# Expert outputs with queries on partitions, router weights as per-partition scalars on VectorE

## What is computed

```python
logits = x @ w_gate                       # 8 experts
w      = top-2 weights, 0 for the others  # one number per token and expert
h      = silu(x @ w1[e]) * (x @ w3[e])    # layers 0, 1, 3 (gated); gelu(x @ up[e]) in layer 2
y     += w[:, e:e+1] * (h @ w2[e])        # layer 3 also adds w @ bias
x      = x + y
```

## Time and profile before

| | |
|---|---|
| median of 3 runs | 4386.78 us |
| the profiled execution, its own time | 4390.38 us |
| its span, first to last instruction | 4388.7 us |
| TensorE busy | 4072.2 us, 93% |
| ScalarE busy | 3859.5 us, 88% |
| VectorE busy | 2842.1 us, 65% |
| GpSimd busy | 819.4 us, 19% |
| mean granted TensorE clock | 0.963 of full |

### The profile page before, as it was taken

The page is one execution under the profiler, slowest core; times in us unless marked ns, Lnnn a source line. Parts: engine busy times, 40 slices in busy tenths (PEclk is TensorE's granted clock), DMA queues, the critical chain, the costliest instruction groups (busy, mean ns, idle before and its releaser), DMA issues.

```text
span 4388.7 us, 69705 instructions
## 1 busy us (share of the span) xinstructions
PE 4072.2 (93%) x26742; PEld 975.0 (22%) x26742; DVE 2842.1 (65%) x5746; ACT 3859.5 (88%) x4328; POOL 819.4 (19%) x705
## 2 busy tenths in 40 slices
PE   8899999999999999999999999899999999999996
PEld 3122222222222222222212222222122221222212
DVE  6889887888977788677503232110685768988813
ACT  3699998999988989898998888889999888999993
POOL 3000003221033211333321111111001110021222
PEclk7699999999999999999999999999999999999998
DMA  5211011100011110111102121110011100010001
GB/s 145 62 29 35 25 31 42 30 18 15 12 47 41 29 30 25 49 35 35 36 16 64 41 64 37 50 41 25 12 29 30 29 15 13 15 35 24 9 6 54
DMA packets 124486, 151.35 MB, mean 34 GB/s; under 512 B 29272, under 2 KB 76384, under 8 KB 124080
## 3 DMA queue, kind: packets, MB, share of 16 engines
q1 hardware_dynamic: 123424, 146.41, 12.6%
q10 hardware_dynamic: 720, 0.40, 0.0%
HBM read 123.21 MB, written 23.51 MB: 33 GB/s over the span
## 4 chain that ended last, share of the span: by engine, by line
PE 58%; ACT 18%; DVE 13%; issue 4%; DMA 1%; SPq 1%; POOL 0%; ACTq 0%; POOLq 0%; DVEq 0%
PE av L1282 24%; ACT prob L1443 14%; PE scores L1272 12%; DVE mpart L1554 9%; PE side L1304 8%; PE scores L1382 5%; PE side L1400 4%; DVE above L1558 2%; PE side L1382 2%; PE scores L1295 1%; ACT above L1451 1%; PE side L1272 1%; DMA cwb<-weights 1%; PE scores L1420 1%; PE scores L1424 0%
## 5 line engine op out<-in xcount | busy, mean ns | idle before, releaser
L1443 ACT ACTIVATE prob<-scores 128x1024 f32<-128x1024 f32 x2999 | 2908.5, 1034 | 180.6 <-PE scores L1272 104.1
L1554 DVE TENSOR_REDUCE mpart<-side 128x1 f32<-128x512 f32 (+1 forms) x3456 | 2077.4, 655 | 451.6 <-PE side L1304 441.5
L1282 PE MATMUL av<-prob,VB 128*9 128x512 f32 x6528 | 873.6, 608 | 0.7 <-ACT prob L1443 0.5
L1282 PE MATMUL av<-prob,VA 128*9 128x512 f32 x6528 | 864.2, 602 | 1.2 <-ACT oS L1461 0.4
L1304 PE MATMUL side<-KA,QP 32*128 32x512 f16 (+1 forms) x2112 | 596.4, 394 | 62.8 <-DVE mpart L1554 39.7
L1272 PE MATMUL scores<-QP,KA 32*128 32x512 f16 x2998 | 577.0, 391 | 46.6 <-ACT prob L1443 30.3
L1272 PE MATMUL scores<-QP,KB 32*128 32x512 f16 x3000 | 573.6, 386 | 33.0 <-ACT prob L1443 19.9
L1558 DVE CUSTOM_DVE_ANT_0 above<-side,above 128x512 f32<-128x512 f32 x768 | 503.6, 687 | 154.0 <-PE side L1304 137.2
L1304 PE MATMUL side<-KB,QP 32*128 32x512 f16 (+1 forms) x2112 | 541.7, 380 | 59.3 <-DVE mpart L1554 32.6
L1451 ACT ACTIVATE above<-scores 128x1024 f32<-128x1024 f32 x383 | 394.4, 1030 | 70.5 <-DVE mpart L1558 41.9
L1272 PEld LDWEIGHTS scores<-QP,KB 32*128 32x128 f16 x3000 | 139.2, 91 | 808.1 <-ACT prob L1443 688.9
(11 more groups left out here) (216 smaller groups left out, 2674.0 us busy)
## 6 DMA issues: line engine op xcount, KB each, us to landing
cwb<-weights SPq DMA_DIRECT2D x80, 256.0 KB, 3.8
KA<-kstacks SPq DMA_DIRECT2D x384, 48.0 KB
KB<-kstacks SPq DMA_DIRECT2D x384, 48.0 KB
Fin<-in_Fin SPq DMA_DIRECT2D x64, 256.0 KB, 2.7
kstacks<-hi SPq DMA_DIRECT2D x100, 128.0 KB, 2.4
ctxc<-in_ctxT SPq DMA_DIRECT2D x36, 256.0 KB, 3.1
hT<-in_mask SPq DMA_DIRECT2D x16, 400.2 KB, 3.5
kstacks<-lo SPq DMA_DIRECT2D x50, 128.0 KB, 2.6
```

The source lines that it names most:

```text
L1282: last = pe.matmul(AV[ROWS * h:ROWS * h + VC, :], V[l % 2][:, kt, g * HG + h, :], prob[:, (e + h // 2) % RING, (h % 2) * QB:(h % 2) * QB + ...
L1443: act.activation(prob[:, e % RING, :], pair.rearrange("p a b -> p (a b)"), ACT.Exp if softmax(l) else ACT.Sigmoid, scale=SCALE).then_inc(s ...
L1554: dve.tensor_reduce(part, bank, AX.X, ALU.max).then_inc(sem["red"], 1)
```

## The change

The downward matmul swaps its operands: a tile of 128 queries of the hidden activations is held and the 128 columns of `Fout` are streamed, four times for the 512 queries, so that `y` has queries on partitions. The router's weight is then one number per partition, and VectorE multiplies and adds straight into the state, in all passes. `cwput`, `cwget`, `xk`, `hscale`, `gatec`, `yc`, `yT`, `yadd` and the buffer in DRAM go. The factor 0.5 moves into the router's small instructions. `cwT` and `cwTc` stay in layer 3 alone, for the biases, which become a product and an addition of their own behind the third expert. The upward matmuls no longer wait for the router: its steps are listed behind the upward steps of the second expert, and the first three fetches of weights ahead of the logits. The last finish takes score banks for the first half of its upward products. The planner's table gains costs for the new steps, and the finish of unit 6 is due at key tile 170 instead of 200. The diff also lets a phase go without differences of key chunks (`DIFS_IN`), but sets two for every phase, as before.

```diff
                 elif s.what == "down":
-                    pe.matmul(bank, Fout[0:fs, w, c, :], h, start=first, stop=c == nk - 1).then_inc(sem["bgP"], 1)
+                    for t in range(QT):
+                        last = pe.matmul(bank[:, t * P:(t + 1) * P], h[:, t * P:(t + 1) * P], Fout[0:fs, w, c, :], start=c + t == 0, stop=(c, t) == (nk - 1, QT - 1))
+                    last.then_inc(sem["bgP"], 1)
+                elif s.what == "bias":
+                    for t in range(QT):
+                        last = pe.matmul(bank[:, t * P:(t + 1) * P], cwT[:, t * P:(t + 1) * P], b2d[:], start=True, stop=True)
...
                 elif s.what == "ysum":
-                        dve.tensor_tensor(yT, yT, bank, ALU.add).then_inc(sem["bgV"], 1)
-                elif s.what == "yadd":
+                    own.wait_ge(*o.sem("routed", u, lp))
+                    for t in range(QT):
+                        last = dve.scalar_tensor_tensor(x[:, t, :], bank[:, t * P:(t + 1) * P], cw[:, t, k:k + 1], x[:, t, :], ALU.mult, ALU.add)
...
-                    if l in (0, 1) and j >= nk:
-                        own.wait_ge(*o.sem("xk", u, lp, k))
-                        x = xk[:, k % 2, :]
+                    own.wait_ge(*o.sem("xTc", u, f"r{lp}" if l == 1 else "f"))
...
+    behind = 1 if f["gated"] else 2
+    for k in range(E + behind):
         for j in range(n):
+            if k < E:
+                out += gated(k, j) if f["gated"] else upward(k, j)
+            if k >= behind and not f["gated"] and not by_dve(u, lp):
+                out += down(k - behind, j)
+        if k == 1:
+            out += route
+        if k >= behind and (f["gated"] or by_dve(u, lp)):
+            out += [s for c in range(n) for s in down(k - behind, c)]
+        if not f["gated"] and k < E and k % 2:
+            out += [Step("ACT", "gelu", (u, lp, i)) for i in (k - 1, k)]
+        if l == 3 and k == BIAS_AT + 1:
+            out += [Step("PE", "cwT", (u, lp)), Step("ACT", "cwTc", (u, lp)), Step("PE", "bias", (u, lp)), Step("DVE", "badd", (u, lp))]
...
+def last_steps():
+
+    return [s._replace(home="pair") if s.what == "up" and s.key[3] < FFN[3]["nk"] else s for s in finish_steps(7)]
...
-FFN_FROM, FFN_TO, KV_FROM, KV_TO = 12, [130, 130, 180, 180, 130, 130, 200], 24, 280
+FFN_FROM, FFN_TO, KV_FROM, KV_TO = 12, [130, 130, 180, 180, 130, 130, 170], 24, 280
```

More of the change, by code:

```diff
@@ L333, in pass_steps @@
-    for k in range(W_RING):
-        out.append((0, Step("SP", "wexp", (u, lp, k))))
-    out.append((0, Step("SP", "cwget", (u, lp, 0))))
-    if f["gated"] and l != 3:
-        out.append((0, Step("POOL", "xk", (u, lp, 0))))
-    out.append((16, None))
-    n = f["nk"]
+    n = f["nk"]
+    out = [Step("SP", "wexp", (u, lp, k)) for k in range(W_RING)] + [Step("PE", "logit", (u, lp))]
+    route = [Step("DVE", what, (u, lp)) for what in ("routea", "routeb", "routee", "routef", "routeg", "routeh")]
@@ L434, in finish_steps @@
         for g in range(NG):
-            out += [(1, Step("PE", "qproj", (u, g))), (0, Step("ACT", "qsplit", (u, g))), (0, Step("POOL", "qadd", (u, g)))]
+            out += [Step("PE", "qproj", (u, g)), Step("ACT", "qsplit", (u, g)), Step("POOL", "qadd", (u, g))]
     else:
-        out.append((2, Step("SP", "out", (b,))))
-    return out
-def placed(at, steps, taken, pace=1.0, together=False):
-    out = []
-    beat = at
-    for gap, s in steps:
-        at += gap
-        if s is not None and s.eng == "PE":
-            if together and s.what == "down" and s.key[-1]:
-                at = before + 4
-            else:
-                at = max(at, int(beat))
-                at += (1 - at) % 4
-                n = FFN[unit(s.key[0])[0]]["nk"] if together and s.what == "down" else 1
-                while any(at + 4 * i in taken for i in range(n)):
-                    at += 4
-                taken.update(at + 4 * i for i in range(n))
-            before = at
-            beat = max(beat, at - 4 * pace) + 4 * pace
-        if s is not None:
-            out.append((at, s))
+        out.append(Step("SP", "out", (b,)))
     return out
@@ L691, in next_maxima @@
         self.p = left[0] if left else None
-        n = len(HALVES[0])
-        self.single = [deque(range(0, n)), deque(range(n, FIRST_BOTH))]
-        self.both, self.dif, self.issued = [deque(), deque()], 0, 0
+        if left:
+            self.single = [deque(singles_of(self.p, half)) for half in range(2)]
+            self.difs, self.singles = deque(difs_of(self.p)), sum(len(x) for x in self.single)
+            self.both, self.issued, self.begun = [deque(), deque()], 0, 0
     def ready(self, s):
-        t = 0.0
-        for k in steps_before(s):
-            if k in self.todo:
-                if k not in self.done:
-                    return None
-                t = max(t, self.done[k])
+        name, t = (s.what, s.key), 0.0
+        if name not in self.before:
+            self.before[name] = [k for k in steps_before(s) if k in self.todo]
+        for k in self.before[name]:
+            if k not in self.done:
+                return None
+            t = max(t, self.done[k])
         return t
@@ L736, in engines @@
                     start = max(best[0], self.free[e])
-                    w = "both" if s.what == "red" and s.key[1] >= FIRST_BOTH else s.what
+                    w = "both" if s.what == "red" and is_both(s.key[1]) else s.what
                     hold = 0.42 * DMAS[w] if e == "SP" else HOLD[e].get(w, USUAL[e])
```

377 lines of the change are left out of this document (138 added, 239 removed).

## The result

The changed kernel takes **4351.73 us** as the median of 5 runs (4347.72 to 4360.89), against 4389.68 (4384.06 to 4397.61) for the kernel before beside it: a ratio of 0.9919, interval 0.9908 to 0.9930. Run again without an edit it took 4360.43, 0.9931 (0.9916 to 0.9947). It is faster by 30 to 38 us; forecast were 4346 us and 40.6 us less. One run of the kernel before, which took 8306 us, is left out of all that follows. The profiled execution took 4359.73 us (span 4358.0), to be held against the 4349.8 that the sum gave.

What follows compares the result with a forecast made beforehand. TensorE was taken to bound phases carrying a finish, ScalarE the last phase without maxima. Terms -14.5 + 5.3 - 13.4 - 13 - 10 + 5 = -40.6 us took the profiled 4390.4 to 4349.8, as a median 4346; range 4312 to 4376.

Steps and rivals of the forecast that it cites:

- 1 tail: Unit 7's uncovered finish: earlier fetches and upward matmuls, a shorter period per expert; -14.5 us, bounds -8 to -19.
- 2 TensorE, hidden: TensorE in the hidden finishes: new downward matmuls cost +5.3 us, removed transposes and their switches give -13.4.
- 3 waits: TensorE's stops at pass starts in layers 0 and 1, plus clock lost behind them, go; -13 us, bounds 0 to -20.
- 4 ScalarE: ScalarE's copies removed, 34 us busy, paid fully only where ScalarE is full; -10 us, bounds 0 to -29.
- 5 VectorE: Each expert's sum as four short VectorE instructions, 0.92 us; a tenth exposed, +5 us, bounds 0 to +46.
- 6 order: Planner's new layout of all instructions and unit 6's earlier due tile; taken as 0, 10 us either way.
- The sign I gave for it: Sign of being wrong: TensorE's idle time behind VectorE grows past 103 us by more than a third.
- phases at 794 to 932 shorter by 2 to 4 us: Sign expected in the new profile: attention phases at 794 to 932 shorten by 2 to 4 us.
- More comes free: Rival: ScalarE's 29 us all on the path and waits bring 20; gain 67 us, 4320 us; chance 0.16.
- Only the tail: Rival: the hidden part comes out even and only the tail's 14.5 us are gained; 4372 us; chance 0.16.
- VectorE's line decides: Rival: in phases with maxima and a finish, VectorE's added 46 us are wholly exposed; +10.4 us, 4397; chance 0.09.
- Weight loads in series: Rival: the downward matmuls' extra weight loads don't overlap; +219 us, near 4560 us; chance 0.01.

Runs made afterwards that it cites:

- e10: Changed kernel with three groups of four 128x128 transposes of a constant added before the last expert's downward matmul in each pass; 4379.30 us, 0.9981 of the kernel before.
- e7: Changed kernel with the downward matmul in its old form, one of 512 columns (output wrong); 4357.82 us, 0.9931 of the kernel before.
- e4: Kernel before, its gate-half upward matmuls in layers 0 and 1 no longer waiting for GpSimd's product (output wrong); 4383.98 us, 0.9988 of the kernel before.
- e3: Changed kernel with 48 idle 512-column ScalarE copies put back, one per expert; 4364.86 us, 0.9936 of the kernel before.
- e5: Changed kernel with each expert's four VectorE sum instructions issued twice and the planner's sum cost raised; 4377.45 us, 0.9977 of the kernel before.
- e6: Changed kernel with one 512-column VectorE sum per expert instead of four, planner cost lowered (output wrong); 4350.28 us, 0.9912 of the kernel before.
- e2: Changed kernel with unit 6's finish due at key tile 200 again instead of 170; 4358.14 us, 0.9921 of the kernel before.
- e9: Changed kernel with the router's steps ahead of all upward matmuls in every pass; 4352.27 us, 0.9919 of the kernel before.
- e11: Changed kernel with only two planner costs edited (downward matmul 0.89, sum 1.1), so another order; 4369.00 us, 0.9962 of the kernel before.
- e8: Changed kernel with the router ahead of the second expert's gates, in the tail alone; 4362.47 us, 0.9936 of the kernel before.

## Why the prediction was right, and by which steps

The median lies in the range, the direction and the likeliest case were right (4352 and 4360 in 4330 to 4362): 30 to 38 us for 40.6. The terms, with what was measured in their place (differences of means, the tail from the trace):

| part | forecast | measured | from |
|---|---|---|---|
| 1 tail | -14.5 | -11.1 | 65.6 to 54.5 us in the trace |
| 2 TensorE, hidden | +5.3 -13.4 = -8.1 | about -14 | e10: -12.9; e7: -1.4 |
| 3 waits | -13 | -4 to -7 | e4 |
| 4 ScalarE | -10 | -7.9 (3 at equal clock) | e3, 6.8 x 56 / 48 |
| 5 VectorE | +5 | about +13, not isolated | e5, e6: a quarter of 53.4 us |
| 6 order | 0 | not separable | e2, e9, e11 |
| sum | -40.6 | -24 to -27 | measured in all: -31.3 |

The measured parts come to within 4 to 7 us of the whole, and each has some 4 us of uncertainty of its own; those of e3, e5 and e6 also hold a new order. At equal clock the same rows give (the tail as it is) -11.1, -4.1, -7.3, -2.9 and +8.5 to +13.9, together -12 to -17, of the 19.4 us that the change brings there. The other 11.9 us go with a clock that rose from 0.9642 to 0.9678. The sum had no term for that but a few us in part 3, and no run shows what raised it. So the total was good in part by luck: parts 1, 3 and 4 were too large, part 5 was most likely too small a loss, and the clock brought what they lacked.

**Part 1.** The working has two slips, of no weight: 4381.3 - 4366.9 is 14.4, and with none of the 6.5 us paid the lower bound is -21 and not -19. It is right in its mechanism, in the 1.8 us and in the period (5.22 for 5.2 to 5.3). The steps mis-sized are "2.5 us for the clock" and "2 us because two experts' gates stand before the router": two gates before the router made the first sum late, TensorE stopped 2.07 us, and its clock fell a second time. e8 and e9 take the stop away, and their tails are 2.3 and 4.8 us shorter. I priced a stop at its length; here it also cost the clock behind it.

**Part 2.** The form cost the 1.09 us forecast. The rule of the Trainium skill that speaks against it, in *TensorE: Matmul & The Clock Gate*, "What overlaps and what doesn't", doesn't hold for these loads, by the rows at 2038.68 and by e7: all of them use the 128 rows, and they overlap. The removed transposes were worth their size, as "a microsecond of TensorE work in a finish costs about a microsecond of time" said: 12.9 us by e10 for the 13.4 forecast, 8.0 at equal clock.

**Part 3.** The step that failed is "in three of the six the clock fell; at half clock 3.4 us do the work of 1.7, so 5", added to the stops. With the stops gone and all else kept (e4) the mean clock did not rise, and the half clock in units 1 to 7 stayed at 157.0 us. So that clock was not to be had by removing the stops; whether one of the three stretches was owed to its stop, one trace can't tell.

**Part 4.** Near to its size as far as e3 tells, with a busy time mis-read: 24.8 us went (3859.5 to 3834.7), not 34, because a copy overlaps the instructions on both its sides, by 0.1 us each; the prediction took 0.1 in all.

**Part 5.** Two errors. The price was 1.13 us an expert, near the upper bound of 1.15 and not the 0.92 chosen: my overlap of 0.06 us came from 512-column reductions. The four starts of a group lie (1.12 - 0.34) / 3 = 0.26 us apart. That is the pace of the prediction's estimate from the Trainium skill, *VectorE: DVE Perf Modes*, "The TRN2 errata"; its total, 1.03 us, is below the 1.12, as the last of the four runs to its end. My nearest row was not near. And the exposed share was taken as a tenth, where e5 and e6 suggest a quarter, without isolating it. The sign I gave for it was blind: TensorE's idle time behind VectorE stayed at 102 us, and in e5 it grew by 10 while the time grew by 20.

**What would show it.** First upward matmul, period, 1.09 us, no stop at a pass's start: as said. State done at 54.5 and not 51. The four instructions: 1.13, not 0.92. And one failed outright: "phases at 794 to 932 shorter by 2 to 4 us". The phase itself takes 140.1 us for 138.0, and unit 1, which holds it, is 10 us longer. A part of that is clock, which fell there from 1.00 to 0.98: with 17.1 us of half clock where there were 3.4, half of the 13.7 is 6.9 us. That is argued from the rows. Why it fell, and what the rest is, stays open: unit 1 is 6.0 us shorter in e9 (clock 0.99) and 5.0 shorter in e6 (0.99), and both have another order there.

**The rivals.** "More comes free" wanted 29 us from ScalarE and 20 from the waits; e3 and e4 give 7 and 4 to 7. "Only the tail": the units are 18.2 us shorter in the trace. "VectorE's line decides": e5 doubled its work and the kernel was still faster than before. "Weight loads in series": e7.

## What to carry to other kernels

In this kernel, whose bounding engine is 93% busy, work added to that engine cost its time in full or nearly. On the engine that is 66% busy beside it, doubled work cost about a quarter of its time, and the table of waits showed only half of that. But a test by doubling must keep the order of the other engines: where a planner lays out all instructions anew, compare the order in the traces, compare runs at equal clock, and test a bare re-ordering before you explain 10 us. An edit of two planner costs moved the time by 13 to 16 us with not one instruction changed.

## What the hardware showed beyond expectation

- One program's runs differ by 17 us in step with the mean granted clock (0.966 to 0.971), 3.3 us for each 0.001. 0.001 of 4358 us is 4.4 us of full clock lost, so three quarters of a lost clock microsecond are paid, by the fit. Part of the spread lies ahead of everything that the change touches: the stretch up to unit 1 takes 647.0 us in the trace of e10 and 654.6 in that of e3.
- The clock falls also where TensorE has made no long stop: in the changed kernel's trace ten low stretches between 800 and 2100 us follow no gap over 0.8 us in its matmuls. One of them, the 8 us before it and its first 3.4 us (TensorE busy for 7.85 of the 8):

```profile
870.90:878.90 8.00, 7.85 (x57) 2.30 (x56) 7.48 (x19) 7.05 (x10) 0.00 (x0) 1.00 0.13 38
878.90:882.30 3.40, 3.40 (x20) 0.47 (x16) 2.43 (x7) 2.62 (x3) 0.00 (x0) 0.51 0.24 61
```

- Whether kinds of work have their own clock stays open. With thirty added transpose groups the mean is 0.9652 for 0.9678, and taking a wait away (e4) did not raise it, 0.9632 for 0.9642. But e8, which differs in the tail alone, has 0.9658, so a difference of 0.002 between sets is chance. The 0.0036 that the change gained, by the fit 12 of its 31 us, is beyond that: 50 runs have 0.9642 and 11 have 0.9678.
- A 128-column `scalar_tensor_tensor` from PSUM with a scalar per partition has a record of 344 ns, and in a row of four the next one starts 0.26 us behind it, so that the four take 1.12 us.
